# Attention with half of its softmax denominators summed by ScalarE, and the maxima turned one third of a product later

## The reference

```python
qkv = x @ w_attn + b_attn
att = einsum('bhqd,bhkd->bhqk', q, k) / sqrt(32)
att = softmax(where(causal, att, -inf), axis=-1)
y = einsum('bhqk,bhkd->bhqd', att, v).transpose(...) @ w_proj + b_proj
```

## Time and profile before

| | us |
|---|---|
| median of 3 runs | 1254.35 (1250.96 to 1254.65) |
| profiled execution, its own time | 1259.87 |
| its span, first to last instruction | 1258.1 |
| of it, attention, to about | 425 |

### The profile page before, as it was taken

The page is one execution under the profiler, slowest core; times in us unless marked ns, Lnnn a source line. Parts: engine busy times, 40 slices in busy tenths (PEclk is TensorE's granted clock), DMA queues, the critical chain, the costliest instruction groups (busy, mean ns, idle before and its releaser), DMA issues.

```text
span 1258.1 us, 20255 instructions
## 1 busy us (share of the span) xinstructions
PE 1186.6 (94%) x6404; PEld 936.4 (74%) x6404; DVE 686.1 (55%) x1485; ACT 454.0 (36%) x699; POOL 281.0 (22%) x405
## 2 busy tenths in 40 slices
PE   7789999999999879999899999999999998999996
PEld 6656676576576558887587888899999997878884
DVE  5465656656657546765366534434334523676744
ACT  3145434434435322322233333244344433233331
POOL 3012313413514311223122540000000001542302
PEclk8889999999999989999999999999999999999998
DMA  7237673522523224334055674345445432655530
GB/s 242 71 102 238 197 258 92 158 83 51 158 62 112 77 98 127 121 120 134 26 81 96 238 252 150 113 135 164 148 136 162 151 102 70 206 176 165 170 118 34
DMA packets 128814, 169.76 MB, mean 135 GB/s; under 512 B 18112, under 2 KB 71360, under 8 KB 128704
## 3 DMA queue, kind: packets, MB, share of 16 engines
q1 hardware_dynamic: 110368, 128.77, 34.3%
q0 software_dynamic: 10336, 32.53, 7.2%
q10 hardware_dynamic: 8000, 7.10, 2.3%
HBM read 95.98 MB, written 47.19 MB: 114 GB/s over the span
## 4 chain that ended last, share of the span: by engine, by line
PE 79%; DVE 7%; DMA 4%; issue 3%; SPq 2%; ACT 2%; ACTq 2%; POOL 1%; POOLq 0%; DVEq 0%
PE bank L852 28%; PE bank L913 17%; PE psT L482 11%; PE bank L1533 3%; PE bank L1534 3%; PE bank L1535 3%; PE psO L587 3%; PE psS L548 3%; PE psN L587 2%; SPq L362 2%; PE psE L569 2%; DVE psS L787 1%; PE bank L1555 1%; PE bank L1578 1%; DMA shared_raw<-in_L_ffn_Sd_dram 1%
## 5 line engine op out<-in xcount | busy, mean ns | idle before, releaser
L913 PE MATMUL bank<-store,shared_held 128*128 128x512 f32 x792 | 188.9, 395 | 3.3 <-issue 2.9
L913 PEld LDWEIGHTS bank<-store,shared_held 128*128 128x128 f32 x792 | 150.2, 190 | 37.5 <-issue 3.3
L482 PE MATMUL psT<-store 128*128 128x512 f32 x576 | 161.1, 415 | 5.3 <-DVE store L701 3.5
L787 DVE CUSTOM_DVE_ANT_0 psS<-psS,attn_mask 128x512 f32<-128x512 f32 (+3 forms) x256 | 121.0, 511 | 61.4 <-PE psS L548 61.3
L657 ACT ACTIVATE acc<-psE 128x512 f32<-128x512 f32 x160 | 93.5, 599 | 144.9 <-PE psE L569 131.6
L482 PEld LDWEIGHTS psT<-store 128*128 128x128 f32 x576 | 108.4, 200 | 25.8 <-issue 4.0
L1447 POOL DMA_INDIRECT routed_rows_io<-sorted_y,routed_pos x32 | 37.2, 1161 | 377.8 <-DMA sorted_y<-routed_rows_io 313.8
L424 POOL TENSOR_SCALAR_AFFINE_SELECT acc<-acc 128x256 f32<-128x256 f32 (+1 forms) x160 | 57.1, 363 | 270.6 <-ACT acc L657 270.2
L852 PE MATMUL bank<-shared_held,routed_h_hi 128*128 x624 | 116.0, 328 | 0.5 <-DVE routed_h_lo L1893 0.3
L852 PEld LDWEIGHTS bank<-shared_held,routed_h_hi 128*128 128x128 f32 x624 | 100.3, 188 | 1.5 <-issue 1.2
L852 PE MATMUL bank<-store 128*128 x351 | 91.5, 405 | 0.0
(11 more groups left out here) (273 smaller groups left out, 2003.2 us busy)
## 6 DMA issues: line engine op xcount, KB each, us to landing
sorted_x<-attn_zero SPq DMA_DIRECT2D x19, 768.0 KB, 6.1
shared_raw<-in_L_ffn_Sg_dram SPq DMA_DIRECT2D x44, 256.0 KB
shared_raw<-in_L_ffn_Su_dram SPq DMA_DIRECT2D x44, 256.0 KB
shared_raw<-in_L_ffn_Sd_dram SPq DMA_DIRECT2D x44, 256.0 KB
routed_rows_io<-sorted_x SPq DMA_DIRECT2D x39, 256.0 KB, 2.9
sorted_y<-routed_rows_io SPq DMA_DIRECT2D x39, 256.0 KB, 2.1
attn_qS<-attn_ch_hi SPq DMA_DIRECT2D x128, 64.0 KB
routed_gu_raw<-in_L_ffn_Wg_dram SPq DMA_DIRECT2D x8, 704.0 KB
```

Of the source, the lines that this page charges most:

```text
L482: last = pe.matmul(out, lhs[a](k), rhs[c](k), start=(s[-1] == 0 and k == 0), stop=(s[-1] == 2 and k == KC - 1))
L787: last = dve.tensor_tensor_reduce(scores, scores, mask[:, (3 - t) * P:T], 1.0, BELOW_ALL, ALU.add, ALU.max, rowmax[:, g % 2, t, i:i + 1])
L913: last = pe.matmul(out, w[:, slot, at + k * P:at + (k + 1) * P], x_part(k), start=(g == 0 and k == 0), stop=(g == 2 and k == KC - 1))
```

## The change

For the last 256 queries (units 0 to 7 of `P1`) the denominators come from ScalarE. VectorE rounds each unit's maxima as the multiplier rows are rounded, and scales them (two instructions on 128x1, each behind a wait for the one before on its own engine). ScalarE takes the exponential of the masked scores in place in `psS`, with that value as its bias, and its accumulator gives the sum of each row (`totals_in`). TensorE's `P1` unit n now waits for `total_done` of unit n-2 instead of `max_done` where n-2 is one of the first eight. GpSimd copies the eight columns of sums out to 32 columns each (`spread`), once a group, behind the mask of `P2` unit 4. Two transposes of 128x128 at the start of `PV` block 0 put them into the right half of `psN`, and the matmuls with ones cover the left half only: 256 columns in block 0, 128 in block 1, none in blocks 2 and 3. `M` moves from behind part 3 of the head to behind part 4. To have semaphores for this, three are merged into others with the same order.

Where ScalarE takes a sum is decided by `totals()`: at `M`, at each `P2`, and at `P1` of unit 9 (for group 0 at each `P1`), it works off the units whose `P1` step has gone by.

```diff
-            if n == 3:
+            if n == 4:
                 steps += [("M", s)]
...
+                    if u == 4:
+                        g = G_
+                        pool.wait_ge(total_done, 8 * (g + 1))
+                        if g:
+                            pool.wait_ge(pv_done, QT * (g - 1) + 1)
+                        pool.tensor_copy(spread[:].rearrange("p n (i d) -> p (n i) d", d=D),
+                                         totals_in[:, g % 2, :].unsqueeze(2).broadcast_to([P, 8, D])).then_inc(spread_done, 1)
...
                     if n >= 2:
-                        pe.wait_ge(max_done, n - 1)
+                        of, was = divmod(n - 2, UNITS)
+                        if was < 8:
+                            pe.wait_ge(total_done, 8 * of + was + 1)
+                        else:
+                            pe.wait_ge(max_done, n - 1)
...
                     pe.wait_ge(max_done, UNITS * (g + 1))
+                    pe.wait_ge(shift_done, 16 * (g + 1))
...
-                    for to, values in ((psO, lambda i: v_f[...]), (psN, lambda i: ones[:])):
-                        for i in range(4):
+                    if j == 0:
+                        pe.wait_ge(spread_done, g + 1)
+                        for n in range(2):
+                            pe.transpose(psN[:, T - (n + 1) * P:T - n * P], spread[:, n, :], ident[:])
+                    for to, values, upto in ((psO, lambda i: v_f[...], T), (psN, lambda i: ones[:], T - 2 * P)):
+                        for i in range(4 if j * P < upto else 0):
...
+            seen, summed = [0], [0]
+            def totals():
+                for n in range(summed[0], seen[0]):
+                    g, u = divmod(n, 8)
+                    scores = psS[:, (g * UNITS + u) % 2, 0:T if u < 4 else T - P]
+                    act.wait_ge(shift_done, 2 * n + 2)
+                    if g >= 2 and u == 0:
+                        act.wait_ge(spread_done, g - 1)
+                    act.activation(scores, scores, ACT.Exp, bias=shift[:, g % 2, u:u + 1], scale=SCALE,
+                                   accum_out=totals_in[:, g % 2, u:u + 1]).then_inc(total_done, 1)
+                summed[0] = seen[0]
...
+                elif kind == "P1":
+                    g, u = s[1:]
+                    if g == 0 or u > 8:
+                        totals()
+                    seen[0] = 8 * g + min(u, 8)
                 elif kind == "M":
+                    totals()
...
                 elif kind == "P2":
+                    totals()
...
                     last.then_inc(max_done, 1)
+                    if u < 8:
+                        dve.wait_ge(max_done, n + 1)
+                        dve.tensor_copy(rounded[:, g % 2, u:u + 1], rowmax[...]).then_inc(shift_done, 1)
+                        dve.wait_ge(shift_done, 16 * g + 2 * u + 1)
+                        dve.tensor_scalar(shift[:, g % 2, u:u + 1], rounded[...].bitcast(F32), -SCALE, None,
+                                          ALU.mult).then_inc(shift_done, 1)
```

More of the change, by code:

```diff
@@ L216, in attention_phase @@
         rowmax = sb("rowmax", [P, 2, QT, 4], F32)
+        rounded = sb("rounded", [P, 2, 8], F32R)
+        shift = sb("shift", [P, 2, 8], F32)
+        totals_in = sb("totals_in", [P, 2, 8], F32)
+        spread = sb("spread", [P, 2, P], F32)
         rsum = sb("rsum", [P, T // D], F32)
@@ L261, in attention_phase @@
         pos_done = sem("pos_done")
-        place_done = sem("place_done")
         w_in = [sem(f"w_in{n}") for n in range(4)]
@@ L280, in attention_phase @@
         max_done = sem("max_done")
+        shift_done = sem("shift_done")
+        total_done = sem("total_done")
+        spread_done = sem("spread_done")
         e_full = sem("e_full")
@@ L407, in _ @@
             drop = pool.to_reg(0.0)
-            pool.wait_ge(consts_ready, 10)
+            pool.wait_ge(consts_ready, 11)
             for n, part in enumerate(kS):
                 if n:
-                    pool.wait_ge(onehot_done, n)
+                    pool.wait_ge(consts_ready, 11 + n)
                 pool.tensor_copy(part[AUX:AUX + 4, :, :],
-                                 onehot[AUX:AUX + 4, :].unsqueeze(2).broadcast_to([4, 4, T])).then_inc(onehot_done, 1)
-            pool.wait_ge(onehot_done, 3)
+                                 onehot[AUX:AUX + 4, :].unsqueeze(2).broadcast_to([4, 4, T])).then_inc(consts_ready, 1)
+            pool.wait_ge(consts_ready, 14)
             for s in steps:
@@ L441, in _ @@
                     if b == 0 and i == 0:
-                        pool.wait_ge(consts_ready, 4)
+                        pool.wait_ge(consts_ready, 5)
                     pool.wait_ge(veps_done, b * QT + i + 1)
@@ L462, in _ @@
         def _(pe):
-            pe.wait_ge(ident_done, 1)
+            pe.wait_ge(consts_ready, 1)
             for _ in range(24):
@@ L506, in _ @@
                     out = take(s)
-                    pe.wait_ge(consts_ready, 10)
+                    pe.wait_ge(consts_ready, 11)
                     pe.wait_ge(sel_done, 1)
@@ L554, in _ @@
                     pe.wait_ge(max_done, UNITS * (g + 1))
+                    pe.wait_ge(shift_done, 16 * (g + 1))
                     for t in range(QT):
-                        last = pe.transpose(out[0:4, t * P:(t + 1) * P], rowmax[:, g % 2, t, :], ident[:])
+                        at = slice(4 * (QT - 1 - t), 4 * (QT - t))
+                        maxima = rowmax[:, g % 2, t, :] if t < QT - 2 else rounded[:, g % 2, at].bitcast(F32)
+                        last = pe.transpose(out[0:4, t * P:(t + 1) * P], maxima, ident[:])
                     give(s, last)
@@ L563, in _ @@
                         if g < 3:
-                            pe.wait_ge(onehot_done, g + 1)
+                            pe.wait_ge(consts_ready, 12 + g)
                     if n >= 2:
@@ L577, in _ @@
                         if g == 0:
-                            pe.wait_ge(consts_ready, 4)
+                            pe.wait_ge(consts_ready, 5)
                         if g:
@@ L583, in _ @@
                                 pe.wait_ge(sh_free[bank_of["V", g // 4, i]], use_of["V", g // 4, i] + 1)
-                    for to, values in ((psO, lambda i: v_f[:, j, (g % 4) * P + i * D:(g % 4) * P + (i + 1) * D]), (psN, lambda i: ones[:])):
-                        for i in range(4):
+                    if j == 0:
+                        pe.wait_ge(spread_done, g + 1)
+                        for n in range(2):
+                            pe.transpose(psN[:, T - (n + 1) * P:T - n * P], spread[:, n, :], ident[:])
+                    for to, values, upto in ((psO, lambda i: v_f[:, j, (g % 4) * P + i * D:(g % 4) * P + (i + 1) * D], T),
+                                             (psN, lambda i: ones[:], T - 2 * P)):
+                        for i in range(4 if j * P < upto else 0):
                             u, c0 = E_AT[j, i]
-                            last = pe.matmul(to[i * D:(i + 1) * D, j * P:T], values(i), p_f[:, u, c0:c0 + (QT - j) * P],
-                                             start=(j == 0), stop=(j == 2), tile_position=(0, i * D))
+                            last = pe.matmul(to[i * D:(i + 1) * D, j * P:upto], values(i), p_f[:, u, c0:c0 + upto - j * P],
+                                             start=(j == 0), stop=(j == (2 if to is psO else 1)), tile_position=(0, i * D))
                     last.then_inc(pv_done, 1)
@@ L695, in _ @@
                 if s == ("Q", 0, 0):
-                    dve.wait_ge(consts_ready, 4)
+                    dve.wait_ge(consts_ready, 5)
                 if kind == "XT":
@@ L722, in _ @@
                     total = counted[:, NT * E:2 * NT * E].rearrange("p (t e) -> p t e", t=NT)
-                    dve.wait_ge(consts_ready, 10)
+                    dve.wait_ge(consts_ready, 11)
                     dve.wait_ge(sh_free[bank_of["CNT",]], use_of["CNT",] + 1)
@@ L762, in _ @@
                     then(dve.tensor_reduce(picked1, picked, AX, ALU.add))
-                    dve.tensor_copy(place[:], picked1).then_inc(place_done, 1)
-                    dve.wait_ge(place_done, 1)
+                    then(dve.tensor_copy(place[:], picked1))
                 elif kind in ("Q", "K") and s[-1] == 2:
```

6 lines of the change are left out of this document (3 added, 3 removed).

## The result

The changed kernel takes 1381.08 us (median of 4 runs, 1379.33 to 1381.26), the kernel before 1252.94 in the same comparison: ratio 1.1013, 95% interval 1.0989 to 1.1037. It is slower, as forecast, but by 128 us where 88 were forecast, and 1381 lies above the range's end of 1376.

What follows compares the result with a forecast made beforehand. TensorE, busy 1186.6 of 1258.1 us, bounds the kernel. 39 + 4 + 6 - 3 + 10 + 3.5 + 2.5 - 2.5 = 59.5, plus 29 for the clock: 88 on 1254.4, 1342 us; range 1297 to 1376.

Steps and rivals of the forecast that it cites:

- The head: `P1` unit 3 waits for unit 1's sum behind ScalarE's four DMA issues; 3.0 us lost in each of 13, 39 us.
- slow issues: In three heads ScalarE's four DMA issues took 3.65 to 4.05 us instead of 2.45 when profiled; 4 us more.
- The clock: Behind each of thirteen heads' standstills TensorE runs 3.4 to 8 us at 0.50, costing 2.2 us each, 29 us.
- The chain: `P1` units 3 to 9 take 8.1 us, not 7.34; 6 us lost in seven iterations without filling, -3 in six with.
- The accumulator: ScalarE's accumulator output costs from nothing up to 0.20 us per sum; 0.1 taken within the hand-over to TensorE.
- rival 2: Accumulator reads of 0.20 us for 128 sums lengthen waits and chains, clock 40 to 45 us: 1365 us, chance 0.17.
- The start: Group 0's `P1` unit 7 waits behind group 1's twelve DMA issues, starting near 57 and not 46.47: +10 us.
- The end: Iteration 14 loses 2.5 us as unit 0's sum precedes `M`'s activation; iteration 15 and the last `PV` save 2.5.
- `M`: Its waits for VectorE's `ch_lo` of `Q`, 8.5 us over 14 groups, go, as more work runs ahead of it.
- The other side: Issues don't hold ScalarE's activations up, so unit 1's sum is ready when `PV` block 0 ends: 1238 us, chance 0.05.
- The clock that holds: TensorE's stalls come but its clock stays up: 1254 + 59.5 = 1314 us, chance 0.17.
- the wash: Stalls half as long and no clock cost: near 1254 us, chance 0.03.

Runs made afterwards that it cites:

- run with work in the wait: Changed kernel with 16 matmuls of 512 columns that nobody reads ahead of `P1` unit 3 in the 13 heads: 1324.44 us, ratio 1.0552 to the kernel before.
- bare wait: Kernel before, no sums, with nine small ScalarE copies behind its issues that `P1` unit 3 waits for in iterations 1 to 13: 1326.49 us, ratio 1.0544.

## Why the prediction was right or wrong

- **The head.** Right: 8.5 us from unit 0 to unit 3 were forecast, 8.56 to 8.84 measured; 3.7 us of standstill forecast, 3.74 to 4.02 measured, 13 times; 45 us and more of waits forecast for them, 50.2 measured, and the order on ScalarE as written. Moving the issues away takes the wait away. Over the 13 heads 39 us were lost. The prediction had 39 and 4 more for slow issues; those didn't come (2.66 to 2.71 us for the four, each time).
- **The clock.** This is the step that failed. The mechanism was right; its size, and the step of pricing chain and clock apart and adding them, were not. The prediction said "I expect 3.4 to 8 us at 0.50 behind each" and put 2.2 us on each head, 29 in all. All thirteen heads paid, and it was 7 to 17 us at 0.50. By the run with work in the wait the clock cost 57 us in all, 48 of them in the 13 iterations (3.7 a head). The bare wait shows that 2.2 us is right where the old `PV` and `P1` follow (28 us for 13). The sums change what follows: units of `P1` two apart are held to the pace of maximum, shift, sum and read, and TensorE has gaps between. In six iterations of the seven without filling the clock is at 0.50 for 17.1 us. So the chain prolongs the low clock. That it does so by these gaps is argued from four runs (short behind bare waits; shorter in two iterations without the reads; low in one iteration without a long wait; low near unit 9 though the wait was filled). No run has the chain's gaps alone.
- **The chain.** 8.1 us forecast from unit 3 to unit 9 at full clock; 7.90 in the run with work in the wait, 8.22 with the issues on SyncE. Right. With the clock low it was 11.1. Without the clock, chain and filling together lost 7.5 us behind the 13 heads, where 6 - 3 = 3 were forecast.
- **The accumulator.** Between 0 and 0.20 us were allowed, by the smallest activation; it is an instruction of its own of 0.195. The forecast took half, rival 2 the whole. Rival 2 also had the clock low until the next head's filling, at 40 to 45 us, which is nearly what came (48); its 1365 is the nearest of the five. Without the reads the kernel is 21 us faster, twice the 9 us of reads that rival 2 counted on the path, and in two iterations the clock is seen back sooner.
- **The start.** +10 forecast, +13.6 measured (unit 0 of group 0 to unit 0 of group 1: 35.85 against 22.25 us). Unit 7 started at 60.26, not near 57: the twelve issues began at 51.91, 4.5 us later than before (47.39), where the prediction had allowed 1.1, as unit 2 waited 3.10 us and unit 4 another 1.45 for their sums.
- **The end.** Iterations 14 and 15 with the last `PV` were put at 0 together; from group 15's unit 0 to the end of the span it is 880.7 against 871.1 us, +9.6. Partly a wrong "nothing": "its reader comes a whole head later" does not hold in the last iteration, which has no head, and GpSimd's copy stood behind four additions of 1.28 us.
- **`M`.** Its wait of 8.5 us went, and alone it brings 10 us.
- **Attention's end and the rest.** Forecast near 510, and the stages after it unchanged. Attention's last product began at 545.1 where it began at 425.3; behind it the span lost nothing to speak of (834.4 against 832.8 us). The end was 35 us late; that nothing after it changed was right.
- **The rivals.** The other side (ScalarE's sums run beside issues) is refuted by the 0.05 us between the last issue and the sum. The clock that holds is refuted, and so is the wash.
- **The sum.** From profile to profile the change cost 121 us, where 88 were forecast. The 13 iterations lost 95 and not 75 (39 + 4 + 6 - 3 + 29), which is the clock (48, not 29) and little else: heads and what follows them, without the clock, were 47 against 46. The start and iteration 0 lost 17 and not 13.5, the end nearly 10 and not 0. So of the 33 us missed some 20 are the clock's and some 13 the two ends'. That heads and chain came out at 47 for 46 is partly luck: the 4 us of slow issues that didn't come made up for the chain's 4 us more.

## What to carry to other kernels

A buffer that is given back later puts its new release behind everything that stands in front of it on the releasing engine; read that engine's order, its DMA issues included, before its busy share (here 36%). Waits of 3 to 4 us were paid for more than once here: in the kernel before a bare 3.3 us made an iteration 5.4 us longer, and in the changed kernel, with 3.9 us and the chain of sums behind them, it was 7.3. So price the clock for what runs behind the wait, not for the wait alone. And before moving an instruction ahead of another, ask who waits for the one that is pushed back. A change in two parts is worth measuring in its parts: here one alone gained 0.8%.

## What the runs showed of the hardware

- ScalarE's accumulator output is a separate ACTIVATION_READ_ACCUMULATOR of 0.19 to 0.20 us, 128 of them.
- An exponential with a per-row bias that reads and writes `psS` takes 659 ns for 512 columns, where the activation with bias into SBUF took 688.
- Sixteen matmuls without use in each of 13 waits made the kernel 57 us faster (1381.08 to 1324.44): TensorE's granted clock stayed up behind unit 3.
- After a wait of about 3.3 us TensorE was at full speed again some 6 us on in the bare-wait kernel (ten of 13 waits), and with the sums' chain only 16 us on (iteration 2 of the kernel without the accumulator).
- Moving four DMA issues a head from ScalarE to SyncE cost 13 us (1245.51 to 1258.16) in a kernel without the sums; 7.3 us of it are seen as waits for late landings.
- Four DMA issues in a row on ScalarE took 2.7 us, and the activation behind them started 0.05 us after their end.
